# A GAT, GCN and LSTM kernel on one core: transposes, gates, joins and the last adds in another order and on other engines

## The reference

```python
h = max(layernorm(x), 0);  x = x + GAT(h, adj)
h = max(layernorm(x), 0);  x = x + L1(h, adj)

def L1(h, adj):
    h = relu(adj @ (h @ Wg0 + bg0))
    h = relu(adj @ (h @ Wg1 + bg1))
    for p in 1..4:                       # skips
        wins = h[:, :nw * p].reshape(B * nw, p, H)      # nw = 256 // p
        last = lstm_last(Wih[p-1], Whh[p-1], biases, wins)
        h[:, arange(nw) * p + p - 1] = last             # the next skip reads it
    return h
```

## Time and profile before

| | before |
| --- | --- |
| three runs, median (lowest, highest) | 451.97 (450.59, 452.68) us |
| the profiled execution, time | 452.38 us |
| its span | 450.5 us |
| TensorE busy | 430.0 us, 95% |
| its weight loads | 371.4 us, 82% |
| VectorE busy | 374.5 us, 83% |
| ScalarE busy | 333.0 us, 74% |
| GpSimd busy | 71.5 us, 16% |
| mean granted TensorE clock | 0.992 of full speed |
| DMA | 11.68 MB, 4.19 MB of it written |

### The profile page before, as it was taken

The page is one execution under the profiler, slowest core; times in us unless marked ns, Lnnn a source line. Parts: engine busy times, 40 slices in busy tenths (PEclk is TensorE's granted clock), DMA queues, the critical chain, the costliest instruction groups (busy, mean ns, idle before and its releaser), DMA issues.

```text
span 450.5 us, 7896 instructions
## 1 busy us (share of the span) xinstructions
PE 430.0 (95%) x2472; PEld 371.4 (82%) x2472; DVE 374.5 (83%) x973; ACT 333.0 (74%) x651; POOL 71.5 (16%) x169
## 2 busy tenths in 40 slices
PE   7689999979999999999999999999999999999995
PEld 6468888878888888888778888899999988887884
DVE  3898999997778877878778888878788789888995
ACT  2579999977899999997777768757767675574552
POOL 5848640422411213110000000000000000000000
PEclk9969999999999999999999999999999999999999
DMA  8910000000000000000000000000000000002116
GB/s 244 324 65 1 2 2 1 0 0 1 1 1 2 0 1 0 0 0 0 1 0 2 1 0 1 0 1 1 1 1 1 1 1 0 1 23 71 47 47 188
DMA packets 14213, 11.68 MB, mean 26 GB/s; under 512 B 1123, under 2 KB 12390, under 8 KB 13926
## 3 DMA queue, kind: packets, MB, share of 16 engines
q1 hardware_dynamic: 11542, 9.97, 7.3%
q10 hardware_dynamic: 2640, 1.33, 1.2%
HBM read 7.10 MB, written 4.19 MB: 25 GB/s over the span
## 4 chain that ended last, share of the span: by engine, by line
PE 70%; DVE 18%; ACT 5%; issue 3%; DMA 2%; DVEq 1%; SPq 0%; ACTq 0%
PE ps L1008 45%; PE ps L1152 12%; PE ps L1156 6%; DVE score L732 4%; DVE score L698 4%; DVE xs L746 2%; DMA xs<-in_x 2%; PE ps L1054 2%; DVE stats L688 2%; ACT v_norm L500 1%; DVE stats L665 1%; PE ps L988 1%; ACT work L625 1%; PE ps L1099 1%; PE ps L1078 1%
## 5 line engine op out<-in xcount | busy, mean ns | idle before, releaser
L625 ACT ACTIVATE work<-ps,bl 128x512 f32<-128x512 f32 (+2 forms) x204 | 111.0, 627 | 26.7 <-PE ps L1156 19.3
L1008 PE MATMUL ps<-h_hi,wl_hi 128*128 128x512 f32 (+3 forms) x252 | 93.5, 371 | 0.9 <-DVE xs L888 0.8
L1008 PE MATMUL ps<-h_hi,wl_lo 128*128 128x512 f32 (+3 forms) x252 | 92.8, 368 | 0.0
L1008 PE MATMUL ps<-h_lo,wl_hi 128*128 128x512 f32 (+3 forms) x252 | 92.7, 368 | 0.0
L615 ACT ACTIVATE work<-work 128x512 f32<-128x512 f32 (+2 forms) x56 | 31.5, 571 | 45.5 <-DVE work L883 34.6
L1008 PEld LDWEIGHTS ps<-h_hi,wl_hi 128*128 128x128 f32 x252 | 47.5, 188 | 8.3 <-issue 1.2
L500 ACT ACTIVATE v_norm<-xs,shift,scale 128x128 f32 (+1 forms) x128 | 53.3, 509 | 1.4 <-POOL shift L409 1.4
L1008 PEld LDWEIGHTS ps<-h_lo,wl_hi 128*128 128x128 f32 x252 | 47.4, 188 | 6.6
L1008 PEld LDWEIGHTS ps<-h_hi,wl_lo 128*128 128x128 f32 x252 | 47.5, 188 | 5.7
L1152 PE MATMUL ps<-s_hi,wl_hi 128*128 128x512 f32 (+2 forms) x144 | 51.7, 361 | 0.0
L1152 PE MATMUL ps<-s_hi,wl_lo 128*128 128x512 f32 (+2 forms) x144 | 51.2, 358 | 0.0
(11 more groups left out here) (127 smaller groups left out, 924.5 us busy)
## 6 DMA issues: line engine op xcount, KB each, us to landing
result<-xs SPq DMA_DIRECT2D x12, 256.0 KB, 2.3
work<-in_w_ih_t SPq DMA_DIRECT2D x1, 1024.0 KB, 10.9
work<-in_w_hh_t SPq DMA_DIRECT2D x1, 1024.0 KB, 9.4
xs<-in_x SPq DMA_DIRECT2D x2, 256.0 KB, 3.6
xs<-in_x SPq DMA_DIRECT2D x1, 512.0 KB, 5.6
result<-xs SPq DMA_DIRECT2D x4, 128.0 KB, 2.4
result<-xs ACTq DMA_DIRECT2D x4, 128.0 KB, 2.8
adj_raw<-in_adj ACTq DMA_DIRECT2D x1, 256.0 KB, 6.8
```

What stands on the lines that cost most here:

```text
L625: nc.scalar.activation(lw[:, par, g, 0:cols], ps[:, 4 * par + g, 0:cols], ACT.Tanh if g == G else ACT.Sigmoid, bias=bl[:, (p - 1) * GATES ...
L1008: ins = nc.tensor.matmul(dst, a, b, start=start and n_ == 0, stop=stop and n_ == 2)
```

## The change

Four edits.

`turned()` on TensorE moves from ahead of stage 1 to between its halves; in ticks without a stage 1 it stays where it was.

The early gates of round 0 become three: I of (0, 0, 0), the round, step and chunk, inside `turned()` of tick 18, ahead of its wait for `y1`; G of (0, 0, 0) and F of step 1, chunk 0, in tick 20. `BEFORE` lists them with the chunk third.

The joins move from VectorE to GpSimd, which does three steps for each chunk of the last two rounds in a row as soon as the first gate of the chunk is made, and counts them in `joined`. TensorE waits for `joined` ahead of the transposes that read them, VectorE ahead of the last round's `result_h`.

In the last round and behind it: `transpose_pair(0)` goes behind the gates of (0, 1) and right ahead of `transpose_pair(1)`; `add_pair(0)` goes from ahead of `result_h(END - 1, 1)` to behind `cell(END, 0, 1)`. Only pair 9 is summed in PSUM. Pairs 10 and 11 are copied out by ScalarE, 10 ahead of the last tanh, and added by GpSimd. Pair 8 is added by VectorE ahead of the last `result_h`, and 12 to 15 behind it. The stores follow in the order 8, 10, 9, 11, then 12 to 15 in halves.

```diff
+        SUMMED = 9
+        COPIED = [10, 11]
+        TURNS = list(range(WITHIN)) + [10, 11, 8, 12, 13, 14, 15]
+        ADDS = [q for q in TURNS if q not in COPIED]
+        WHOLE = list(range(WITHIN)) + [8, 10, 9, 11]
+        HALVED = [12, 13, 14, 15]
...
+            for r in (END - 1, END):
+                for par in range(2):
+                    pool.wait_ge(c_gate[par], gate_base[r] + 1)
+                    for k in range(LAST - 1):
+                        hi, lo = (window_cols(h, r, par, k).bitcast(fp32) for h in (h_hi, h_lo))
+                        done(to_result(r, par, k, lambda to, run: nc.gpsimd.tensor_tensor(to, run(hi), run(lo), ALU.add)))
+                    nc.gpsimd.nop().then_inc(joined, 1)
+            for n_, q in enumerate(COPIED):
+                pool.wait_ge(e_copy, n_ + 1)
+                xq = xs[:, q * 4:q * 4 + 4, :].rearrange("p k f -> p (k f)")
+                nc.gpsimd.tensor_tensor(xq, xq, copied(q), ALU.add).then_inc(e_sum, 1)
...
-            cell_tanh(len(ROUNDS) - 1, LAST - 1, 1)
-            for n_, q in enumerate(SUMMED):
-                act.wait_ge(e_sum, n_ + 1)
...
+            def copy_out(q):
+                act.wait_ge(d_T, TURNS.index(q) + 1)
+                nc.scalar.activation(copied(q), ps[:, bank_out(q), :], ACT.Copy).then_inc(e_copy, 1)
+            copy_out(10)
+            cell_tanh(END, LAST - 1, 1)
+            copy_out(11)
+            act.wait_ge(e_res, 1)
...
             def result_h(r, par):
                 acts(r, LAST - 1, par, 5)
+                if r == END:
+                    dve.wait_ge(joined, 2)
...
                 full_h(r, 0, 0)
-                if r == END:
-                    add_pair(0)
...
-                        if p == LAST and k > 0:
-                            join(r, k - 1, par)
                         if r == END and (k, par) == (0, 1):
+                            add_pair(0)
                             add_pair(1)
...
+            add_pair(8)
             result_h(END, 1)
-            for q in range(WITHIN, PAIRS):
-                if q not in SUMMED:
-                    add_pair(q)
+            for q in HALVED:
+                add_pair(q)
...
-                        pe.wait_ge(wl_ok, 2)
-                        for s in range(1, 4):
-                            pe.wait_ge(b_lo[s], PAIRS)
-                        pe.wait_ge(one_lo, 4)
-                        for g in (I, G):
-                            gate_of_window(0, 0, 0, g, True).then_inc(c_gate[0], 1)
+                        pe.wait_ge(b_y, PAIRS)
+                        gate_of_window(0, 0, 0, G, True).then_inc(c_gate[0], 1)
+                        pe.wait_ge(b_lo[2], PAIRS)
+                        gate_of_window(0, 1, 0, F, False)
...
+                    if isinstance(t, int) and t == PAIRS + 2:
+                        pe.wait_ge(wl_ok, 2)
+                        pe.wait_ge(b_lo[1], PAIRS)
+                        pe.wait_ge(one_lo, 4)
+                        gate_of_window(0, 0, 0, I, True).then_inc(c_gate[0], 1)
                     pe.wait_ge(b_y, t - 2)
...
                 for s in (4, 3, 2, 1):
-                    if s == 1:
-                        turned()
                     if not live(s):
+                        if s == 1:
+                            turned()
                         continue
...
                         for b in range(2):
+                            if (s, b) == (1, 1):
+                                turned()
...
-                        if r == END:
+                        if r == END and (k, par) != (0, 0):
                             q = 2 * k + par
-                            if q in (0, 4):
+                            if q in (1, 4):
                                 pe.wait_ge(c_h[q // 4], h_base[r])
+                                pe.wait_ge(joined, q // 4 + 1)
...
+                            if q == 1:
+                                transpose_pair(0)
                             transpose_pair(q)
...
-            residual(8)
             pe.wait_ge(c_h[0], h_total)
-            sum_pair(8)
-            residual(9)
-            sum_pair(9)
+            pe.wait_ge(joined, 3)
             transpose_pair(10)
             pe.wait_ge(d_out, WITHIN)
             transpose_pair(11)
+            transpose_pair(8)
+            residual(SUMMED)
+            sum_pair(SUMMED)
             pe.wait_ge(c_act[1], a_total - 1)
-            residual(15)
             pe.wait_ge(c_h[1], h_total)
-            transpose_pair(12)
-            sum_pair(15)
-            transpose_pair(13)
-            transpose_pair(14)
+            pe.wait_ge(joined, 4)
+            for q in HALVED:
+                transpose_pair(q)
```

More of the change, by code:

```diff
@@ L219, in preln_gat_gcn_lstm_kernel @@
         c_lo = [sem(f"c_lo{q}") for q in range(2)]
+        joined = sem("joined")
         d_T = sem("d_T")
         d_out = sem("d_out")
+        e_res = sem("e_res")
+        e_copy = sem("e_copy")
         e_sum = sem("e_sum")
@@ L271, in preln_gat_gcn_lstm_kernel @@
         WITHIN = PAIRS // 2
-        SUMMED = [8, 9, 15]
-        HALVED = [12, 13, 15, 14]
-        def added(q):
-            if q in SUMMED:
-                return e_out, SUMMED.index(q) + 1
-            return d_out, q + 1 - sum(e < q for e in SUMMED)
+        SUMMED = 9
[4 more added lines that the diff above has]
+        HALVED = [12, 13, 14, 15]
+        def added(q):
+            if q == SUMMED:
+                return e_out, 1
+            if q in COPIED:
+                return e_sum, COPIED.index(q) + 1
+            return d_out, ADDS.index(q) + 1
         def bank_out(q):
@@ L287, in bank_out, with copied @@
             return [G, F, O, I][q - WITHIN] if q < WITHIN + 4 else q - WITHIN
+        BEFORE = [(0, 0, 0, I), (0, 0, 0, G), (0, 1, 0, F)]
+        def copied(q):
+            return lw[:, 0, (I, G)[COPIED.index(q)], :]
         def steps_of(r):
@@ L347, in wl, with to_result @@
             return wl_of[part][(p - 1) // 2][:, (p - 1) % 2, m, :]
+        def to_result(r, par, k, ins_of):
+            to = result_of[chunk_of(r, par) // 8].rearrange("f (c b t) -> f c b t", c=4, b=2)
+            for q in range(3):
+                run = slice(2 * RUN[q], 2 * (RUN[q] + RUNS[q]))
+                ins = ins_of(to[:, :, :, 4 * q + k:N:12],
+                             lambda v: v[:, :, run].rearrange("f c (a b) -> f c b a", b=2))
+            return ins
         block = ctx.enter_context(nc.Block())
@@ L365, in store @@
                 sp.dma_start(out_v[:, q * 4 + lo:q * 4 + hi, :], xs[:, q * 4 + lo:q * 4 + hi, :]).then_inc(stored, 16)
-            for q in range(PAIRS - len(HALVED)):
+            for q in WHOLE:
                 store(q, 0, 4)
@@ L846, in part_lo @@
                                         ).then_inc(c_lo[par], 1)
-            def to_result(r, par, k, ins_of):
-                to = result_of[chunk_of(r, par) // 8].rearrange("f (c b t) -> f c b t", c=4, b=2)
-                for q in range(3):
-                    run = slice(2 * RUN[q], 2 * (RUN[q] + RUNS[q]))
-                    ins = ins_of(to[:, :, :, 4 * q + k:N:12],
-                                 lambda v: v[:, :, run].rearrange("f c (a b) -> f c b a", b=2))
-                return ins
             def result_h(r, par):
                 acts(r, LAST - 1, par, 5)
+                if r == END:
+                    dve.wait_ge(joined, 2)
                 o, tc = (like_window(lw[:, par, n_, :], r, par) for n_ in (O, R_TC))
@@ L861, in result_h @@
                           ).then_inc(c_h[par], 1)
-            def join(r, k, par):
-                hi, lo = (window_cols(h, r, par, k).bitcast(fp32) for h in (h_hi, h_lo))
-                to_result(r, par, k, lambda to, part: nc.vector.tensor_tensor(to, part(hi), part(lo), ALU.add))
             def cell(r, k, par):
@@ L885, in add_pair @@
             def add_pair(q):
-                dve.wait_ge(d_T, added(q)[1])
+                dve.wait_ge(d_T, TURNS.index(q) + 1)
                 xq = xs[:, q * 4:q * 4 + 4, :].rearrange("p k f -> p (k f)")
@@ L1126, in _ @@
                         for g in gates:
-                            if (r, k, par) == (0, 0, 0) and g in (I, G):
+                            if (r, k, par, g) in BEFORE:
                                 continue
```

6 lines of the change are left out of this document (3 added, 3 removed).

## The result

The change makes the kernel slower: 461.96 us median (461.73 to 462.27, 4 runs) against 451.36 (4 runs) for the kernel before. The profiled execution took 461.73 us with a span of 459.5, against 452.38 and 450.5 before. I had forecast 452.8, in a range that ended at 456.0.

The account below looks back on a forecast made before the run. TensorE, or a chain pacing it, was taken as the bound, with stores setting the end; +0.6 - 0.15 + 1.2 - 0.8 = +0.85 on the profiled 452.38 us, which lay 0.4 above the median: forecast 452.8, range 450.0 to 456.0.

Parts of the forecast that it names:

- The joins: Last two rounds: 36 instructions of 0.48 us leave VectorE; TensorE waits for none of them, so gain 0.
- rival B: Last two rounds: GpSimd's joins hold VectorE's two-SBUF-input instructions; +3.8 us, 456.6 us in all; chance 0.22.
- the one row of before: GpSimd beside VectorE at 99.98: GpSimd took 0.67 us (median 0.20), VectorE its usual 0.69; read as VectorE first.
- The order in the last round: `add_pair(0)` moved later: F gate starts at 404.7, not 402.59; net +1.2 us.
- the 0.77 us wait: Last round: TensorE's wait at 408.20 for VectorE's add of pair 2, forecast to vanish with the new order.
- behind it TensorE is the bound, so it stays: Last round, behind the F gate's wait: the net +1.2 us loss carries through.
- The transposes: GCN pipeline, between stage 1's halves: start delayed, tick stays 7.25 us; net +0.6 us, between 0 and +1.3.
- the marks: Signs: first `y1` transposes behind the table load near 127.9, 7.25 us ticks, first `s_hi` product near 233.2.
- The early gates: Entry to LSTM rounds: early I gate fills TensorE's 0.78 us wait at 219.11; gain 0.15 us, at best 0.68.
- The tail: Program's end: fewer PSUM sums, earlier late stores, end at 448.8 against 449.6; gain 0.8 us, between 0.5 and 1.4.
- ahead of need: Tail: GpSimd's adds of pairs 10 and 11, up to 1.5 us each, done by 441.0 and 442.7.
- the lower bound: Tail: gain of 0.5 us from the first late store alone, issued near 440.6 instead of 441.09.

Follow-up runs that it names:

- order_only: Kernel before with only pair 0's transposes and add moved behind the cell of half 1 in the last round; 454.98 us, ratio 1.005.
- order_filled: order_only with TensorE repeating the three G gate products three times, thrown away, to fill its wait; 453.4 us, ratio 1.0017.
- turned_only: Kernel before with only the `y1` transposes moved between the halves of stage 1; 452.52 us, ratio 1.0001.
- tail_and_gates: The change without its joins on GpSimd and without pair 0's new place; 456.23 us, ratio 1.0077 against the kernel before.
- add0_early: The change with pair 0's transposes and add back in their old places; 462.34 us, ratio 1.0187 against the kernel before.
- after_filled: The change with the G gate's three products repeated eight times, thrown away, in the last round; 460.63 us, ratio 1.0189 against the kernel before.
- tail_alone: Kernel before plus early gates and new tail, GpSimd's additions and pair 8's add held behind `result_h`; 453.71 us, ratio 1.0021.
- joins_copy: joins_only with each GpSimd join only copying the high part, one SBUF input instead of two; 453.8 us, ratio 1.0016 against the kernel before.
- joins_only: Kernel before with only the 36 joins moved to GpSimd, with the waits they need; 462.45 us, ratio 1.0219.

## Why the prediction was wrong

**The joins: the step that failed.** I put them at 0, since "TensorE waits for none of them", and gave what they do to VectorE a chance of 0.22 at a price of 3.8 us. Measured alone they cost 8.3 us up to the last product, 2.5 in one round and 5.8 in the other. Two errors lie in it. The first is the question: TensorE waits for no join, but it waits for every `s_hi` and `s_lo`, and in the last round for the additions, and so for whatever makes VectorE slower. The second is the size of rival B. I took 0.51 us, the estimated length of a join, for each of nine instructions and then half of it, and a third for the round before, since the one row of before had VectorE first. Beside a queue of joins VectorE is seldom first: the engines go in turn, and nearly every instruction of VectorE with two SBUF inputs pays. Between 400.16 and the F gate these are six at 0.44 and the three pieces of `result_h` at 0.38 (0.74, 0.68 and 0.67 apart instead of 0.31), 3.8 us, where I had 2.3; only the `s_lo` of 408.08, which started just ahead of a join, went free. In the round before I had 1.5, and it was 2.5. The slow clock behind the waits I had not at all. The rule of the Trainium skill that the prediction names under rival B (page SBUF — State Buffer, section Who interferes with whom), with a row that agrees, deserved the higher chance.

**The order in the last round.** The wait came as worked out: F gate 2.1 us late (2.08 in order_only), the 0.77 us wait gone, +1.12 net against +1.2 (order_filled). The mis-sized part is what I left out: "behind it TensorE is the bound, so it stays". Behind the wait TensorE runs at its lower level for 3 to 4 us, +1.5 us; in the change, with 5.2 us of wait, 2.6.

**The transposes** cost 0.67 (forecast 0.6), with the marks at 128.04 (127.9), 7.26 us a tick and 233.30 (233.2). **The early gates** bring 0, forecast 0.15.

**The tail** brings 0.53 in the change, forecast 0.8. The first store comes 0.57 us sooner, as foreseen (0.5); VectorE's last addition doesn't come 1.4 sooner but, measured from the last product, exactly when it did (8.72), because GpSimd's additions hold `result_h`. The gain also leans on the joins: with them back on VectorE the same tail costs 2.3 us. I had called GpSimd's additions free by their end ("ahead of need") and not asked what ran beside them. Of C the whole length was set by the first store, which I had as the lower bound and should have had as the value.

**The sum.** By stretch the +8.94 of the trace are 0.63 (transposes, as in turned_only), 0.09 (gates, by tail_and_gates), 1.86 (the rest of A, the joins in the round before the last, 2.5 when measured alone), 6.9 (last round) and -0.5 (tail). Only the first two were measured apart; the others are the change's own stretches, so that they add up is no check. In the last round 2.6 are the clock, 1.1 the new order as measured alone, and the 3.2 left over are put down to the joins; these three aren't independent, as add0_early shows (the order is worth 1.0 with the joins, 2.7 without). The medians of the result are 10.6 us apart, the profiled executions 9.35: that of before lay 1.0 above the 451.36 and that of after 0.2 below its median.

No version tried beats the kernel before. The one part that gains is the tail of the change, 0.5 us, and only with VectorE free of joins; on GpSimd they cost more than that.

## What to carry to other kernels

Before work moves to GpSimd, list what VectorE executes beside it: here nearly every VectorE instruction with two SBUF inputs paid some 0.4 us beside GpSimd instructions with two, and the price is TensorE's if VectorE feeds it. Price a new wait of TensorE by its length plus the slow products behind it (1.5 us behind a wait of 2.1 us here), and look whether work without a dependence can fill it. Where stores set the end, ask when the first of them starts, not when the last result is ready.

## What the runs showed of the hardware that I had not expected

- VectorE and GpSimd, both with two SBUF inputs: VectorE's 0.69 us becomes 1.07 to 1.14 where a join runs already, the starts go from 0.61 to 1.04 us apart, and GpSimd's addition of 168 elements goes from 0.64 us alone (in after_filled, at 417 us) to 0.95 in the mean. Where VectorE starts first it keeps its 0.68 us and the addition takes 1.15. VectorE's addition with one input in PSUM stays at 0.68. A GpSimd addition of 512 elements turns a VectorE instruction of 0.45 us into one of 1.5.
- GpSimd's copy, one SBUF input, adds some 0.12 us to the same VectorE instructions, and takes 0.90 us itself instead of 0.50 beside them.
- TensorE kept its upper level behind waits of 0.8, 1.3 and 1.5 us (tail_alone, joins_copy, joins_only), and fell to the lower behind those of 2.1, 3.5 and 5.2 us (order_only, joins_only, after), for 3 to 6 us. Waits filled with products that were thrown away kept it. The length of the wait isn't all: behind the wait of 3.5 us in the tail of tail_and_gates the transposes stood 0.11 us apart, as at the upper level, and the granted clock fell only 1.2 us later, at 448.9.
